# The scan's large products inside its score tiles: where the g projection and the output products stand on TensorE

## The reference, cut to what matters

```
def step(state, rkvw):
    r_t, k_t, v_t, w_t = rkvw
    a = k_t[..., :, None] * v_t[..., None, :]
    y = jnp.einsum('bhk,bhkv->bhv', r_t, state + u[None, :, :, None] * a)
    new_state = w_t[..., :, None] * state + a
    return (new_state, y)
...
g = jax.nn.silu(xg @ Wg)
_, ys = jax.lax.scan(step, state0, (r_, k_, v_, w_))
...
return yn.reshape(Bb, Tt, Cc) * g @ Wo
```

## Time and profile before

| what | value |
|---|---|
| median of three runs | 4667.7 us (4663.5 to 4677.39) |
| profiled execution, its own time | 4653.57 us |
| its span | 4652.0 us |
| TensorE busy | 3940.7 us (85%) |
| VectorE busy | 3757.0 us (81%) |
| ScalarE busy | 1374.0 us (30%) |
| GpSimd busy | 1389.0 us (30%) |
| mean granted TensorE clock | 0.913 |

### The profile page before, as it was taken

How to read it: one execution, slowest core, us unless ns; L and a number is a source line. 1 busy time by engine, 2 the same in 40 slices (tenths; PEclk the granted TensorE clock), 3 DMA queues, 4 the chain that set the end, 5 groups by cost and what they waited for, 6 DMA issues and landing times. The chain is left out here.

```text
span 4652.0 us, 152262 instructions
## 1 busy us (share of the span) xinstructions
PE 3940.7 (85%) x64712; PEld 2646.2 (57%) x64712; DVE 3757.0 (81%) x7929; ACT 1374.0 (30%) x2555; POOL 1389.0 (30%) x735
## 2 busy tenths in 40 slices
PE   4888888989988888989898713889999989999988
PEld 3777676767767676777677502444444444444444
DVE  4877777777767777877777577899999999999997
ACT  2434342433334342424333112122222222222221
POOL 1112212121111212121211125444444444444443
PEclk7999998999989999999989856899999999999999
DMA  3000000000000000000000020001001001001000
GB/s 104 17 26 17 30 16 21 25 22 26 21 26 16 25 22 22 25 22 25 21 26 12 21 98 18 19 27 34 27 27 34 27 27 34 27 27 34 27 27 27
DMA packets 72856, 131.36 MB, mean 28 GB/s; under 512 B 12705, under 2 KB 13473, under 8 KB 72290
## 3 DMA queue, kind: packets, MB, share of 16 engines
q1 hardware_dynamic: 72290, 123.00, 8.3%
HBM read 89.43 MB, written 33.55 MB: 26 GB/s over the span
## 5 line engine op out<-in xcount | busy, mean ns | idle before, releaser
L712 POOL TENSOR_TENSOR xf<-xf,hT 128x1024 f32<-128x1024 f32 x128 | 309.5, 2418 | 1196.5 <-DVE xf L762 1196.5
L878 DVE COPY_PREDICATED Am<-pick,banks 128x64 f32<-128x64 uint8 (+2 forms) x1792 | 460.6, 257 | 125.5 <-DVE Am L878 8.6
L1525 PE MATMUL fbank<-gT,xqT 128*128 128x464 f16 (+1 forms) x2304 | 536.7, 387 | 15.8 <-DVE h L1384 13.6
L1525 PE MATMUL fbank<-uT,xqT 128*128 128x464 f16 (+1 forms) x2304 | 488.2, 362 | 0.0
L1547 PE MATMUL fbank<-dT,hqT 128*128 128x512 f16 x2112 | 477.4, 380 | 0.2 <-ACT hqT L1460 0.2
L723 POOL TENSOR_TENSOR yrs<-yvar,neg_half 128x32 f32<-128x32 f32 x32 | 174.0, 5437 | 888.0 <-DVE yvar L907 888.0
L1474 ACT ACTIVATE sil<-fbank,und 128x464 f32<-128x464 f32 (+1 forms) x192 | 125.1, 651 | 913.0 <-PE fbank L1525 913.0
L1525 PEld LDWEIGHTS fbank<-gT,xqT 128*128 128x128 f16 x2304 | 237.0, 105 | 275.6 <-issue 57.6
L1525 PEld LDWEIGHTS fbank<-uT,xqT 128*128 128x128 f16 x2304 | 225.7, 98 | 232.1 <-issue 1.9
L1341 POOL TENSOR_TENSOR hq<-q16h,s16h 128x1408 f16<-128x1408 f16 x64 | 210.5, 3288 | 445.4 <-DVE s16h L1331 445.4
L762 DVE SCALAR_TENSOR_TENSOR xf<-banks,col_maa,sx 128x256 f32<-128x256 f32 x640 | 265.3, 477 | 87.9 <-PE banks L462 86.6
(11 more groups left out here) (230 smaller groups left out, 8701.0 us busy)
## 6 DMA issues: line engine op xcount, KB each, us to landing
x_tok<-in_L_attn_x SPq DMA_DIRECT2D x32, 512.0 KB, 3.9
xres<-in_L_attn_x SPq DMA_DIRECT2D x32, 512.0 KB, 3.6
x_after_attention<-xres SPq DMA_DIRECT2D x32, 512.0 KB, 3.6
xl<-x_after_attention SPq DMA_DIRECT2D x64, 256.0 KB, 2.7
xr<-x_after_attention SPq DMA_DIRECT2D x64, 256.0 KB, 2.7
out<-xr SPq DMA_DIRECT2D x64, 256.0 KB, 2.0
raw_g<-in_L_wmod SPq DMA_DIRECT2D x3, 1024.0 KB, 5.2
raw_g<-in_L_ffn_w_gate SPq DMA_DIRECT2D x1, 2816.0 KB, 10.3
```

Of the source, the lines that this page charges most:

```text
L712: nc.gpsimd.tensor_tensor(xf[:, j % NXF].rearrange("p g b t -> p (g b) t"), xf[:, j % NXF].rearrange("p g b t -> p (g b) t"), hT[:, :, :, ...
L878: nc.vector.copy_predicated(dst, mask, src).then_inc((done or A_step).sem, 1)
L1525: last = nc.tensor.matmul(GU[2 * pair + t][:, 0:w], xqT[:, u, a, g, :], W[:, b_, g, lo_:hi_], start=(k == 0), stop=(k == 3 * G - 1))
```

## The change

The same products are computed with the same operands. `pe_scores` takes a list `between` of up to two functions: the first is called behind the 16 products of 32x80, the second ahead of the 16 `kT` products. `pe_g` now does one channel group (4 products of 128x256) a call, and `pe_wo` half a batch (2 products of 128x512). Groups 0 and 1 of g stand inside score tile 1, groups 2 and 3 inside score tile 2. The output product's halves stand inside the score tiles 4 and 5 (batch 0) and 6 and 7 (batch 1), each behind the 16 products of 32x80. The waits go with the first product of their pair: `gu_done` with group 2, `x1_done` of batch 0 with the first half of batch 1. Lines of the new file behind L403 are 2 to 8 higher than before (L404, the products of 32x80, keeps its number).

```
-        def pe_scores(pe, c, n):
+        def pe_scores(pe, c, n, between=()):
...
                     nc.tensor.matmul(sc[d, g * NS:(g + 1) * NS], kvar[d, 0, g, b, 32 * q:32 * q + 32], rcol[d, X, 0:M1], start=True, stop=True)
+            for large in between[0:1]:
+                large()
...
+            for large in between[1:2]:
+                large()
             if n == 0:
                 settled_after(pe, mod_done, (vT_done, c), (kT_done, c))
...
-        def pe_g(pe, c, h, do_p):
-            if h == 0:
+        def pe_g(pe, c, g, do_p):
+            if g == 0:
...
-            else:
+            elif g == 2:
                 after(pe, gu_done, c, 1)
-            for g in (2 * h, 2 * h + 1):
...
+            if g % 2:
+                last.then_inc(proj_done.sem, 1)
...
+        def pe_wo(pe, f, b, half, fenced, gated):
+            if half == 0:
+                after(pe, z_done, f)
...
+                if b == 1:
+                    after(pe, x1_done, f, 1)
+            for k in (2 * half, 2 * half + 1):
                 last = nc.tensor.matmul(SMALL[:], yn[:, k, b, :], w_o[:, b, k, :], start=(k == 0), stop=(k == G - 1))
-            last.then_inc(wo_done.sem, 1)
+            if half:
+                last.then_inc(wo_done.sem, 1)
...
             for n in range(1, 8):
+                between = []
+                if n <= 2 and do_w:
+                    between = [lambda g=g: pe_g(pe, c, g, do_p) for g in (2 * n - 2, 2 * n - 1)]
+                elif n >= 4 and do_f:
+                    between = [lambda: pe_wo(pe, f, (n - 4) // 2, n % 2, do_p, do_w)]
                 if do_w:
-                    pe_scores(pe, c, n)
-                    if n <= 2:
-                        pe_g(pe, c, n - 1, do_p)
+                    pe_scores(pe, c, n, between)
                     pe_y(pe, c, n - 1)
...
-                if n == 4 and do_f:
-                    pe_wo(pe, f, 0, do_p, do_w)
...
-                if n == 6 and do_f:
-                    pe_wo(pe, f, 1, do_p, do_w)
```

More of the change, by code:

```diff
@@ L504, in pe_g @@
                     after(pe, mf_done, c + 1)
-            else:
+            elif g == 2:
                 after(pe, gu_done, c, 1)
-            for g in (2 * h, 2 * h + 1):
[L508 to L520, removed]
-            for k in range(G):
+            for k in range(G):
+                last = nc.tensor.matmul(SMALL[:, (g % 2) * BT:(g % 2 + 1) * BT], w_g[:, k, g * P:(g + 1) * P],
+                                        xf[:, NMIX - 1, k].rearrange("p b t -> p (b t)"), start=(k == 0), stop=(k == G - 1))
+            if g % 2:
[3 more added lines that the diff above has]
+                after(pe, z_done, f)
+                if b == 0 and fenced:
+                    after(pe, u1_done, f + 2)
+                elif b == 0 and gated:
+                    after(pe, gu_done, f + 1)
+                if b == 1:
+                    after(pe, x1_done, f, 1)
+            for k in (2 * half, 2 * half + 1):
                 last = nc.tensor.matmul(SMALL[:], yn[:, k, b, :], w_o[:, b, k, :], start=(k == 0), stop=(k == G - 1))
-            last.then_inc(wo_done.sem, 1)
+            if half:
+                last.then_inc(wo_done.sem, 1)
         def pe_body(pe, i, do_p, do_w, do_f, more, more2):
@@ L527, in pe_body @@
             for n in range(1, 8):
+                between = []
[3 more added lines that the diff above has]
+                    between = [lambda: pe_wo(pe, f, (n - 4) // 2, n % 2, do_p, do_w)]
                 if do_w:
-                    pe_scores(pe, c, n)
-                    if n <= 2:
-                        pe_g(pe, c, n - 1, do_p)
+                    pe_scores(pe, c, n, between)
                     pe_y(pe, c, n - 1)
+                else:
+                    for large in between:
+                        large()
                 if n == 3 and do_p:
```

## The result

The changed kernel took 4811.7 us in the median of four runs (4795.3 to 4818.6), beside 4672.6 us for the kernel before on the same chip: a ratio of 1.029, 95% interval 1.025 to 1.033. It is slower, by 139 us; the forecast was 177 us more, 4845 us in a range of 4765 to 4940. The profiled execution's span is 4803.6 us against 4652.0, 151.6 us more.

What follows compares the result with a forecast made beforehand. The lead of TensorE's score tiles was taken to keep VectorE running and so bound the scan. Terms of 4.1 + 3.1 - 0.9 - 0.6 gave +5.7 us a chunk, +177 us over 31 bodies: 4845 us, range 4765 to 4940.

Steps and rivals of the forecast that it cites:

- The mechanism: In score tiles 2 and 6 TensorE stands waiting for `gu_done` and `x1_done`, released late by VectorE, which waits in turn.
- Term A: A 1 to A 2: TensorE's wait for `gu_done` inside score tile 2 delays A 2, +4.1 us a chunk.
- Term B: A 5 to A 6: batch 1's first output half waits for VectorE's addition inside tile 6, +3.1 us a chunk.
- Term C: Between A 2 and A 6: the mix behind A 2 no longer waits for its delta, -0.9 us a chunk.
- Term D: A 6 to A 7: TensorE still decides, needing about 6.1 us instead of 6.65, -0.6 us a chunk.
- I take no change: TensorE's granted clock in the scan: taken as unchanged, with bounds of 0 and +3 us a chunk.
- Rival 1: Steps 1 to 7: even mixing removes issue stalls and clock drops, moved waits met in time; 4544 us, chance 0.05.
- the issue stalls: TensorE's "issue" idle pieces amid small products, up to 6.7 us a chunk, which mixing in large products might remove.
- The changes of product size: TensorE switching between large and small products: 0.1 us a visit, bounds 0 to 0.2, counted only on the path.

Runs made afterwards that it cites:

- z_early: The changed kernel with VectorE's z moved ahead of A 1: 4653.5 us, ratio 1.0010 to the kernel before.
- out_early: The changed kernel with VectorE's addition of batch 0 moved from behind the fifth mix to ahead of A 5: 4673.8 us, ratio 1.0064.
- both_early: The changed kernel with VectorE's z ahead of A 1 and its addition of batch 0 ahead of A 5: 4516.7 us, ratio 0.9717.

## Why the prediction was right, point by point

- The mechanism was right: both waits were in the trace, 31 times each, released by the operations named. TensorE's stand before group 2 was forecast at 3.2 us and is 3.22 in the chunk shown (3.1 in the mean). `z_early` and `out_early` show that each wait had its price on the path.
- Term A was mis-sized: +5.9 us instead of +4.1. In the chunk shown A 1 came at 719.00, 1.2 us late in place of 1.1 (1.6 in the mean). The wait was right. What was missing is the clock behind it: group 2 took 3.44 us instead of 1.86 (3.1 in the mean).
- Term B, the same: +5.6 instead of +3.1. From the addition's end to A 6 it is 5.54 us in place of 3.0; the half took 3.75 us instead of 1.8 (3.6 in the mean).
- Term C: -1.4 instead of -0.9. The mixes' idle time for their delta products (L762, now L770) fell from 75.6 us over the scan to 13.7.
- Term D was wrong by most: -4.3 instead of -0.6. I worked it out in a chunk at full clock, in which A 6 to A 7 takes 6.65 us. The mean chunk took 11.0 there. In the mean of the 29 chunks td2 took 3.3 us and the whole output product 5.1, against 1.97 and 3.60 at the full clock, which is 2.9 us of the 4.35 missing; where the rest lies was not looked into. After the change A 6 to A 7 is 6.7 us; 6.1 was forecast.
- "I take no change" for the clock was the step that failed. As a balance over the chunk it was nearly true (11.2 us at the lower clock before, 13.3 after), but it hid more loss behind each wait (1.3 to 3.8 us up to A 2, 1.1 to 7.2 before A 6) and less in step 6 (6.0 to 0.6). All four terms came out too small in size: the two losses by 1.8 and 2.5 us, the two gains by 0.5 and 3.7, and 0.9 more came back behind A 7. These errors nearly cancel. So the mechanism was understood, but that the total came out so well, 5.7 against 5.0 us a chunk, was luck.
- Rival 1 was not the outcome, but its gain is real: with both waits out of the way the same TensorE order is 2.8% faster than before. Its other half, the issue stalls, was given back in the changed kernel too (7.7 to 4.2 us a chunk), while the new waits grew by more; what the stalls are worth by themselves was not measured.
- The changes of product size: 14 visits instead of 8 could cost 0.1 us each. `both_early` has all 14 and gains 132 us, so they are no large cost; a size of their own was not measured.

## What to carry to other kernels

When work of one engine is put earlier in its order, look at the wait that comes with it: which engine releases it, and whether that engine is waiting for what now stands behind the wait. If so, move the releasing operation earlier too (here moving two lines for each of the two waits made a loss of 2.9% a gain of 2.8%), or leave the wait behind the result that the other engine needs. Here the gain came with spreading the output product over four steps; standing inside a tile added nothing, and behind the tiles it was fastest. And a reference chunk at full clock shows the order of events but not the mean cost; take the price of a term from the mean of its stretch over all chunks.

## What the runs showed of the hardware

TensorE's "issue" gaps amid small products are not random. Counting all of TensorE's records in the trace (weight loads, products, its sequencer's), the gaps of over 0.9 us in one lap of the loop of the kernel before (31,763 records, 38 such gaps) stand all but one at the same count modulo 256, within one. They end 2.2 to 2.9 us behind the start of a 16 KB transfer on the instruction queue. The one exception is the turn of the loop, 3.5 us. The same count comes 124 times in the lap; in the 63 cases in which 24 or more of the 255 records before it belong to large products, no gap there is over 0.5 us. The Trainium skill (Runtime: NRT & Kernel Launch, Instruction fetch mechanics) says that instructions are fetched in blocks of 16 KiB, 256 instructions, and that crossing a block is mostly hidden; this trace agrees with the block, but the crossing is not hidden where nearly all products are of 32 rows and columns and start some 0.02 us apart (32 of them in 0.76 us): there it shows gaps of 0.9 to 2.4 us. That a late fetch causes them is inferred from the count and from the transfers. The issue gaps of over 0.3 us are 7.7 us a chunk; how much of the chunk hangs on them is left open above.
